# A spectral convolution on one core: the batch blur ahead of the channel mix cut down to six of eight images

## The reference

```
x = L0(x)                            # 3x3 filter per image, from its means
x_ht = dht_2d(x)                     # keep [:20, :20]
out_ht[:, :, :20, :20] = compl_mul2d(x_ht, w1)   # mix channels, per mode
y = dht_2d(out_ht) / (H * W)
for ax in range(4):                  # ax 0 is the batch
    y = blur_axis(y, ax, gauss(sigma=1, radius=4))
return y * mask                      # |column frequency| <= 0.25
```

## Time and profile before

| | |
|---|---|
| median of 3 runs | 151.29 us (150.51 to 154.11) |
| the profiled execution | 149.94 us |
| its span, first to last instruction | 147.9 us |
| TensorE busy | 122.4 us (83% of the span) |
| VectorE, ScalarE, GpSimd busy | 58.4, 35.8, 38.9 us |
| read from HBM, written to it | 20.22 MB, 16.78 MB |

### The profile page before, as it was taken

One profiled execution on the slowest core, in us unless ns is written; L12 is line 12 of the kernel. 1 busy time (PEld: TensorE's weight loads), 2 busy tenths in 40 slices (PEclk: granted clock), 3 DMA queues, 4 the chain that ended last, 5 costly groups with the idle time before them and its releaser, 6 DMA issues.

```text
span 147.9 us, 5730 instructions
## 1 busy us (share of the span) xinstructions
PE 122.4 (83%) x2574; PEld 71.2 (48%) x2574; DVE 58.4 (39%) x119; ACT 35.8 (24%) x85; POOL 38.9 (26%) x21
## 2 busy tenths in 40 slices
PE   6757587999998899999789399999995999978300
PEld 5513233545453545455558297666563565543100
DVE  1033843464645465464327720343341443342200
ACT  3000410111110111111305612534332444233100
POOL 8999000405555190919350000000000000000000
PEclk9999999999999999999999999999999999999965
DMA  4999999999999999200000000079999999999996
GB/s 109 350 361 276 370 353 348 349 394 350 391 354 359 354 353 343 91 4 0 4 0 7 0 4 4 4 246 333 339 345 339 337 342 343 340 342 336 347 343 235
DMA packets 34438, 37.35 MB, mean 252 GB/s; under 512 B 800, under 2 KB 33824, under 8 KB 34416
## 3 DMA queue, kind: packets, MB, share of 16 engines
q1 hardware_dynamic: 34272, 36.94, 75.7%
q10 hardware_dynamic: 144, 0.07, 0.4%
HBM read 20.22 MB, written 16.78 MB: 250 GB/s over the span
## 4 chain that ended last, share of the span: by engine, by line
PE 54%; DMA 21%; SPq 10%; ACT 4%; issue 3%; DVE 2%; DVEq 0%
PE ps L556 16%; DMA x_ring<-x 16%; PE ps L373 10%; DMA out<-rows 5%; PE ps L535 4%; PE ps L515 4%; PE ps L390 4%; PE ps L361 3%; PE ps L495 3%; SPq L334 3%; ACT mixin L610 3%; SPq L315 3%; PE ps L426 2%; SPq L322 2%; PE ps L445 2%
## 5 line engine op out<-in xcount | busy, mean ns | idle before, releaser
L373 PE MATMUL ps<-x_ring,k_wide 64*64 64x512 f32 x256 | 31.2, 602 | 6.9 <-DMA x_ring<-x 6.9
L713 DVE STREAM_TRANSPOSE y_sb<-ps 128x1024 f32<-128x1024 f32 x16 | 20.0, 1250 | 31.5 <-PE ps L373 31.5
L556 PE MATMUL ps<-cols,k_wide 128*64 128x330 f32 (+1 forms) x192 | 30.4, 464 | 0.7 <-ACT rows L585 0.7
L585 DVE COPY rows<-ps 128x330 f32<-128x330 f32 (+1 forms) x24 | 12.6, 525 | 19.6 <-PE ps L556 17.0
L556 PEld LDWEIGHTS ps<-cols,k_wide 128*64 128x64 f32 x192 | 13.2, 136 | 13.5 <-issue 4.7
L373 PEld LDWEIGHTS ps<-x_ring,k_wide 64*64 64x64 f32 x256 | 8.3, 132 | 20.9 <-issue 12.3
L857 POOL TENSOR_TENSOR spread<-parts,k_wide 128x960 f32<-128x960 f32 (+2 forms) x6 | 10.1, 1688 | 23.6 <-ACT parts L637 23.6
L585 ACT COPY rows<-ps 128x330 f32<-128x330 f32 (+1 forms) x24 | 11.0, 463 | 18.7 <-PE ps L556 13.0
L361 PE MATMUL ps<-idle 128*128 128x256 f32 x46 | 13.5, 442 | 1.2 <-DVE idle L704 1.2
L390 PE MATMUL ps<-y_sb,k_wide 64*64 64x96 f32 x512 | 14.2, 248 | 0.0
L859 POOL TENSOR_TENSOR acc<-acc,spread 128x960 f32<-128x960 f32 (+2 forms) x6 | 12.6, 2093 | 0.5
(11 more groups left out here) (59 smaller groups left out, 93.4 us busy)
## 6 DMA issues: line engine op xcount, KB each, us to landing
x_ring<-x SPq DMA_DIRECT2D x16, 1024.0 KB, 12.0
out<-rows SPq DMA_DIRECT2D x16, 640.0 KB, 6.0
out<-rows SPq DMA_DIRECT2D x8, 768.0 KB, 7.5
w_sb<-mix_w SPq DMA_DIRECT2D x2, 960.0 KB, 12.3
k_wide<-wide SPq DMA_DIRECT2D x1, 528.0 KB, 11.8
k_tab<-narrow SPq DMA_DIRECT2D x1, 361.2 KB, 10.0
k_wide<-wide SPq DMA_DIRECT2D x1, 354.0 KB, 12.1
k_wide<-wide SPq DMA_DIRECT2D x1, 128.0 KB, 5.7
```

The costliest lines, as they stand in the source:

```text
L373: last = nc.tensor.matmul(ps[64 * t:64 * t + 64, 2 * g + e, :], k_wide[rows_in, O_LT + 64 * r:O_LT + 64 * r + 64], x_ring[rows_in, u, 8 * ...
L556: last = nc.tensor.matmul(ps[64 * g:64 * g + 64, B_F[k % 3], 0:nt * NW], const(O_LH + s * H + r * H // 2, (1, H // 2)), cols[:, u, 6 * g:6 ...
L585: return copy(view(rows[:, u, s, r, 0:1], (3 * 2 * H, nt), (H - HALF, 2), (1, HALF)), view(ps[:, B_F[k % 3], 0:1], (NW, nt), (HALF, 2), (1 ...
L713: nc.vector.transpose(view(y_sb[:, g, 0, 0, 0:1], (1, 1024)), view(ps[:, 2 * g, 0:1], (1, 1024))).then_inc(y_out, 1)
```

## The change

The blur ahead of the mix covers images 0 to 5 only (`EARLY = 6`). Images 6 and 7 go through the mix raw, as two further columns behind the eight, so the mix has ten columns for each of its 8 groups (`NCOL = 10`, 80 instead of 64 in all) and fills four PSUM banks, six modes to a bank. Their shares in outputs 2 to 7 are added behind the mix, in `mixed`, by DVE: eleven steps, each waiting for the one before, spread over the output stage. Since `acc` is complete once image 5 is added, the copies from `acc` to `mixin` are moved into the chain of image 7. The raw sums of images 6 and 7, with a negated copy that `keep_parts` makes, are placed by GpSimd (all of image 6 and one quarter of image 7), ACT (two quarters of image 7) and DVE (one quarter). `keep_busy` ahead of the mix goes from 8 calls to 3, and the 2 calls behind the mix are left out.

```diff
+    EARLY = 6
+    NCOL = N + N - EARLY
+    PER_BANK = 512 // (2 * J * NCOL)
...
-        B_TURN, B_MIX = 1, 5
+        B_TURN, B_MIX = 1, (0, 5, 6, 7)
...
-            keep_busy(8)
+            keep_busy(3)
...
+            pe.wait_ge(placed, N - EARLY)
+            pe.wait_ge(placed_dve, 1)
+            pe.wait_ge(placed_act, 1)
...
             def turn(n):
+                if shared_at[n] > 0:
+                    pe.wait_ge(share_step, shared_at[n])
...
-            keep_busy(2)
             pe.wait_ge(gaps_zero, 1)
-            pe.wait_ge(mixed_dve, 1)
-            pe.wait_ge(mixed_act, 1)
+            pe.wait_ge(mixed_dve, 2)
+            pe.wait_ge(mixed_act, 2)
             turn(0)
...
+        def place_raw(copy, n, j):
+
+            part, at = slice(C * j, C * j + C), N + n - EARLY
+            return copy(view(mixin[part, 0, j, 0, at:at + 1], (NCOL, 3), (J * 3 * NCOL, HALFP)),
+                        parts[part, n % 2, :, :])
...
             def keep_parts(n):
                 act.wait_ge(sums_done, n + 1)
...
+                if n >= EARLY:
+                    done = nc.scalar.mul(parts[:, n % 2, 2, :], ps[:, B_SMALL, AT_SUM:AT_SUM + HALFP], -1.0)
+                done.then_inc(parts_done, 1)
...
+            act.wait_ge(parts_done, N)
+            place_raw(nc.scalar.copy, N - 1, 0)
+            place_raw(nc.scalar.copy, N - 1, 1).then_inc(placed_act, 1)
+            for i in range(2):
+                act.wait_ge(mix_done, 2 * i + 1)
+                unmix(nc.scalar.copy, 2 * i).then_inc(mixed_act, 1)
...
+            def add_shares(n):
+
+                for k in range(EARLY, N):
+                    if weight[n, k]:
+                        if steps[0]:
+                            dve.wait_ge(share_step, steps[0])
+                        steps[0] += 1
+                        nc.vector.scalar_tensor_tensor(
+                            mixed[:, n, :, 0:MODES], mixed[:, N + k - EARLY, :, 0:MODES], float(weight[n, k]),
+                            mixed[:, n, :, 0:MODES], op0=ALU.mult, op1=ALU.add).then_inc(share_step, 1)
...
+            add_shares(0)
+            add_shares(1)
+            cols_step(0, 0)
+            add_shares(2)
+            for n in range(N):
+                rows_step(n, n % 2, n // 2, (1,))
+                if n + 1 < N:
+                    cols_step(n + 1, (n + 1) % 2)
+                if n + 3 < N:
+                    add_shares(n + 3)
+                rows_step(n, n % 2, n // 2, (3, 5))
...
-            for n in range(N - 1):
+            for n in range(EARLY):
                 spread_step(n)
+            pool.wait_ge(zeroed, 2)
+            for n in range(EARLY, N):
+                pool.wait_ge(parts_done, n + 1)
+                for j in (range(J) if n < N - 1 else (J - 1,)):
+                    last = place_raw(nc.gpsimd.tensor_copy, n, j)
+                last.then_inc(placed, 1)
```

More of the change, by code:

```diff
@@ L261, in hartley_conv_kernel @@
         kb = sb("kb", [KROWS, C])
-        parts = sb("parts", [128, 2, 2, HALFP])
+        parts = sb("parts", [128, 2, 3, HALFP])
         spread = sb("spread", [128, N, PLANE])
@@ L588, in unmix @@
         def unmix(copy, bank):
-            b0, nb = bank * 8, min(8, MODES - bank * 8)
-            copy(view(mixed[:, 0, 0, b0:b0 + 1], (BPAD, J), (S * J * BPAD, N), (1, nb)),
-                 view(ps[0:Q * C, B_MIX + bank, 0:1], (2 * N, J), (1, N), (2 * J * N, nb)))
+            b0, nb = bank * PER_BANK, min(PER_BANK, MODES - bank * PER_BANK)
+            step = 2 * J * NCOL
+            copy(view(mixed[:, 0, 0, b0:b0 + 1], (BPAD, J), (S * J * BPAD, NCOL), (1, nb)),
+                 view(ps[0:Q * C, B_MIX[bank], 0:1], (2 * NCOL, J), (1, NCOL), (step, nb)))
             skip = 0
@@ L634, in keep_parts @@
                 act.wait_ge(sums_done, n + 1)
[L635 to L638, removed]
+                if 1 < n:
+                    act.wait_ge(acc_done, min(n - 1, EARLY))
+                if n - 2 >= EARLY:
+                    act.wait_ge(placed, n - 1 - EARLY)
+                done = nc.scalar.copy(view(parts[:, n % 2, 0, 0:1], (1, PLANE)),
+                                      ps[:, B_SMALL, AT_SUM:AT_SUM + PLANE])
+                if n >= EARLY:
+                    done = nc.scalar.mul(parts[:, n % 2, 2, :], ps[:, B_SMALL, AT_SUM:AT_SUM + HALFP], -1.0)
+                done.then_inc(parts_done, 1)
             act.wait_ge(setup, 1)
@@ L647, in _ @@
                     keep_basis(n - 1)
+                    if n == N - 1:
+                        act.wait_ge(acc_done, EARLY)
+                        act.wait_ge(zeroed, 2)
+                        place_minus_odd(0)
                     keep_parts(n - 1)
                 filters(n)
+            place_minus_odd(1)
+            place_minus_odd(2)
             keep_basis(N - 1)
+            place_minus_odd(3).then_inc(mixin_act, 1)
             keep_parts(N - 1)
[L653 to L662, removed]
+            act.wait_ge(parts_done, N)
[4 more added lines that the diff above has]
+                unmix(nc.scalar.copy, 2 * i).then_inc(mixed_act, 1)
             def modes_step(n, u):
@@ L785, in _ @@
             turn_columns(N - 1)
+            dve.wait_ge(acc_done, EARLY)
+            dve.wait_ge(zeroed, 2)
+            place_sums(0)
+            place_sums(1)
             products(N - 1)
-            dve.wait_ge(acc_done, N - 1)
+            place_sums(2)
+            place_sums(3).then_inc(mixin_dve, 1)
             dve.wait_ge(parts_done, N)
[L790 to L800, removed]
+            place_raw(nc.vector.tensor_copy, N - 1, 2).then_inc(placed_dve, 1)
             for quad in range(4):
@@ L805, in _ @@
             last.then_inc(gaps_zero, 1)
-            dve.wait_ge(mix_done, 2)
-            unmix(nc.vector.tensor_copy, 1).then_inc(mixed_dve, 1)
+            for i in range(2):
+                dve.wait_ge(mix_done, 2 * i + 2)
+                unmix(nc.vector.tensor_copy, 2 * i + 1).then_inc(mixed_dve, 1)
+            dve.wait_ge(mixed_dve, 2)
+            dve.wait_ge(mixed_act, 2)
+            steps = [0]
+            def add_shares(n):
[7 more added lines that the diff above has]
+                            mixed[:, n, :, 0:MODES], op0=ALU.mult, op1=ALU.add).then_inc(share_step, 1)
             def cols_step(n, u):
```

34 lines of the change are left out of this document (19 added, 15 removed).

## The result

The changed kernel takes 149.59 us, the median of 20 runs (148.04 to 152.66), beside 152.13 us of the kernel before in the same sessions (20 runs). The ratio is 0.9863 with a 95% interval of 0.9825 to 0.9900: 1.4% faster, some 2.1 us, where 3.8 us were forecast. The profiled execution took 148.38 us with a span of 146.6 us, 1.6 and 1.3 us less than before.

A forecast was written before the change was run, and what follows sets the result against it. The stores set the end, so the chain ahead of the first store bounds the kernel. Gains of 4.4 and 0.6 us less 1.2 us make 3.8 us, from 151.29 to 147.5 us; range 145.2 to 149.7 us.

The forecast's parts named there:

- Part 1: Ahead of the mix: with only raw copies left behind image 7's sums, the mix starts 4.4 us earlier.
- Rival 1: Ahead of the mix: raw copies are slow, 1.09 us each, so the kernel takes 148.9 us; chance 0.18.
- Part 2: In the mix: 80 columns instead of 64 make it longer, 5.88 instead of 4.70 us, a loss of 1.2 us.
- Part 3: From the mix to `turn`: without idle calls `turn` follows the last copies, 0.63 instead of 1.26 us, gain 0.6 us.
- Rival 3: In the mix: with fewer idle calls TensorE's clock falls to 1.2 GHz and the kernel takes 153.4 us; chance 0.05.
- Part 4: In the output stage: DVE's added shares, 0.7 us a pair, hide in 0.94 us of idle time, costing nothing.
- Rival 2: In the output stage: shares cost 1.05 us each and delay stores, nearly undoing the gain, about 150.5 us; chance 0.06.

The follow-up runs named there:

- b_idle: The kernel before with only the cut in idle matmuls (8 calls to 3 ahead of the mix, 2 to none behind it): 152.19 and 153.57 us.
- b_pad112: The kernel before with 56 tiny unused matmuls (112 matmul instructions) added at two places in PE's waits for data: ratio to before 1.015.
- a_pad60: The changed kernel with 30 tiny unused matmuls (60 matmul instructions) added behind the first half of image 0's stage1: 151.1 us, ratio to before 1.0024.
- after: The changed kernel itself, first profile: 149.59 us median, ratio to before 0.9863.
- after_again: The changed kernel, unaltered, run and profiled once more: ratio to before 0.9933.

## Why the prediction was wrong, point by point

**Part 1 (4.4 us) held.** The mix starts 4.31 us earlier. `parts_done` rose at 78.49 us; image 7 ran 0.2 us ahead of the profile before, so the forecast of 78.7 us was met. A raw copy took 0.52 us on ACT and GpSimd and 0.47 us on DVE, where I took 0.35 on ACT: ACT's two ended at 79.57 instead of 79.4 us, and PE waited 0.32 us behind its idle calls. Rival 1 is out: its 1.09 us a copy is twice the measured. (71.52 + 1.09 us is 72.61, not 72.64 us; nothing hangs on it.)

**Part 2 (1.2 us) held for the work.** Without a stop the mix takes 5.78 to 6.04 us, 1.1 to 1.3 us more than 4.70. In the changed kernel it takes 6.56 us, 1.86 us more, with the stop of 0.49 us in it: over the 6.5 us that the prediction named as its sign of being wrong.

**Part 3 (0.6 us) held.** From the mix to `turn` of image 0 it is 0.51 instead of 1.26 us. It was argued as if the idle calls there had no other use; that the clock stays at 1.00 without them was right, and the standstill ahead of the mix had gone as well. `b_idle` shows the same cut where the standstill stays and grows: 7.46 us for the mix. Rival 3 has a bound and a reading wrong. It was to decide only from a standstill longer than the 2.39 us in the earlier trace rows, but in `b_pad112` the clock fell behind one of 2.40 us. And the mean of 0.97 in the earlier trace rows shows no fall where PE waits for the stores: the granted clock was 1.00 from 98 to 141 us and 0.57 from 141 to 144 us, behind PE's last matmul at 137.7 us.

**Part 4 (nothing) held.** A pair of shares took 0.67 us, and DVE idled 0.29 us behind it instead of 0.94 us; leaving the shares out changed neither the stops nor, within 0.4 us, the time. Rival 2 is out as I put it.

**The step that failed** is the first: "Whatever comes off this chain ahead of 89.99 us moves every store forward, as long as nothing is added between `turn` and the stores." I looked for added instructions there and found none. What was added is PE's wait for its own code: from `turn` to the first store 7.09 instead of 5.73 us, and a stop in the mix ahead of it. The forecast had the first store 3.8 us earlier, and it is 1.84 us. Against `a_pad60`, which does the same work without a stop in this stretch, the mix takes 0.8 us more and the way from `turn` of image 0 to the first store 1.2 us more (7.09 against 5.87): together the 2.0 us that are missing. The rows' 0.49 and 0.97 us are less than that because they count from the end of the last matmul, which lasts some 0.2 us in the profile, while without a stop the next one starts after some 0.02 us. Some 0.2 of the 1.2 us are lost in `turn` of image 0. In the profile before, the idle calls and the standstill ahead of the mix looked like pure waste. They were also the time in which a block of code came in ahead of a dense stretch of small matmuls. The view that could have said so, the queue of instruction DMAs on the page, I did not read, and "issue" rows between matmuls of one line, such as 1.54 us at 112.60 us in the chain before, I took for harmless because the stores queue there.

**The last 0.5 us** are between the first store and the end: 52.7 instead of 52.2 us. In the profile of `after` PE stops 0.8 to 1.6 us in each of images 4 to 7 of the output stage; before, it stops twice, 1.54 and 0.91 us. These stops too end 2.3 to 2.4 us behind a burst, so that their lengths hang on when the burst comes. That differs between runs of one kernel: `after_again` has the first of the four alone, and the granted clock at 0.50 from 114.2 to 117.6 us. I can't say which of them the end rests on. The median of 149.59 us lies inside the range of 145.2 to 149.7 us by luck: the range was made of bounds on the copies, the mix and the way to `turn` and of the spread of the runs, and the wait that took the gain is in none of them. Left open is also which point of the code sets off the request; it was bounded between the 7th and the 16th matmul instruction behind the sums of image 7, and its lead was not measured elsewhere.

## What to carry to other kernels

Before a wait on TensorE is taken out, look at what else happens in it: here it let the next block of code come in. Where a stretch has hundreds of small matmuls, count instructions as well as columns, and read "issue" stops every 256 instructions as missing code; a shift of the code by a few cheap instructions ahead of a wait tests it, and may be the cure: here it took the stop out of the mix. A shift also moves the stops of all later stages, so look at the whole span.

## What the runs showed of the hardware

- TensorE's code arrives during the run in blocks of 16 KB, some 256 instructions. In the quiet stretch the stops for a block ended 2.3 to 2.9 us after the start of its packet (all kept profiles), under the load of the stores 2.2 to 2.5 us; when PE stopped for one after the other the bursts were 4.0, 4.1 and 3.8 us apart (80.55, 84.55, 88.65 and 92.45 us in the changed kernel). At 25 ns a matmul instruction with its load, the mix uses up a block in 3.1 us.
- The granted clock after the same standstill of 2.4 us was 1.00 in the kernel before and fell to 0.50 in `b_pad112`, 1.3 us into the mix; after 4.55 us in `b_idle` it was 0.50 from the first matmul of the mix on. It also fell to 0.50 within the output stage of some profiles (`after_again`, 114.2 to 117.6 us) and not of others of the same kernel (`after`, 1.00 until 141.9 us).
